# Small products of a linear-attention layer: full-width per tile, or in 32-column tiles once a sequence

## The chip, the cores and the metric

The kernel runs on one core of one Trainium2 chip. The metric is device time in microseconds; the profile is of one execution on that core. The engines are TensorE (PE in the rows; PEld is its weight load), VectorE (DVE), ScalarE (ACT), GpSimd (POOL) and SyncE (SP).

## What is computed

16 sequences of 512 tokens, width 256, float32, go through one layer: attention with 16 heads of width 16 and no softmax over positions, a residual and a layer norm, then a gated feed-forward network of width 704 with block-quantized weights and activations, again with residual and norm. The attention, cut to what matters:

```python
q = favor(x @ Wq + bq)          # per head: exp(x - max) / (sum + EPS)
k = favor(x @ Wk + bk)
v = x @ Wv + bv
numerator = einsum('bhld,bhmd->bhlm', q, k)
attention_probs = numerator / (sum(q) + EPS)
context = einsum('bhlm,bhmd->bhld', attention_probs, v)
return context @ Wo + bo
```

Since nothing nonlinear stands between the two einsums, a head's context is q times a 16x16 matrix, the sum over the sequence's tokens of k features by values. That matrix is what the change is about.

## The kernel before

Tokens are cut into 64 tiles of 128, four (T) to a sequence. Every engine runs one hand-written program: a loop over steps m, in each of which it does its share of several tiles, each of them at another stage; the order within a step is written out in code, and engines meet at semaphores only (`need(engine, semaphore, count)`). Attention runs in steps up to about 70, one tile a step; the preparation of the feed-forward weights runs beside it in 18 pieces; then the feed-forward loop (`ffn`) follows, starting while the last tiles of attention end.

A tile n in attention goes as follows. TensorE projects it to query and key (`query_key`, step n, 6 products of 512 columns in L820) and to values (6 of 256 columns). VectorE takes the head maxima (L682) and subtracts them (L720), ScalarE takes the exponential (L513) and re-seeds the PSUM bank with the bias (L449), VectorE sums and inverts (L692, L707), GpSimd multiplies into query and key features (L376). ScalarE copies the values out of PSUM (L540). In step n + 3 TensorE waits for features and values, transposes the 256 query features (L851, two transposes of 128 columns), and multiplies values by key features (L853): for each of two chunks of 128 features a product of 128 x 128 over the tile's 128 tokens, accumulated in the bank `pkv` over the four tiles. Only the blocks of 16 x 16 on the diagonal are of use. Once a sequence VectorE multiplies `pkv` by a mask that keeps them (L711, result `kv_m`), and TensorE multiplies that by Wo (L882), which ScalarE and VectorE split into two parts (L521, L696). In step n + 7 TensorE multiplies the transposed query features by the result (L820, 6 products into `wide`), and VectorE adds the residual (L667).

In VectorE's program L711 stands in step 4q + 5 for sequence q, ahead of the subtraction (L720) of that step's tile; in TensorE's, the last L853 of sequence q is in step 4q + 6, at its start, followed by a weight piece's transposes (L865) if there are any, the output projection of an earlier tile, `query_key`, L882 and the value projection.

Features (`feat`, query and key beside each other) and values (`v_sb`) have two buffers each. GpSimd (L375) and ScalarE (L539) wait with tile n until TensorE has ended the products of tile n - 2.

Of the kernel before, what the change touches and what calls it, by code (L numbers as in the profile page):

```python
# [32 lines left out]
P = 128  # L33
# [3 lines left out]
FEPS = 1e-6  # L37
LN_EPS = 1e-5
TINY = 1e-12
SHY = 1.0 + 2.0 ** -22  # L40
NEWTON = 3
BOWL = (4.0 / 3.0) ** 0.5
# [17 lines left out]
def layer_kernel(nc, x_tok, x_feat, Wq, bq, Wk, bk, Wv, bv, Wo, bo, w_ffn, I, out):  # L60
# [16 lines left out]
    with ExitStack() as ctx:  # L77
# [28 lines left out]
        wf_hi = sb("wf_hi", [P, KC, NW * P], F32R)  # L106
        wf_lo = sb("wf_lo", [P, KC, NW * P], F32R)

        SCRATCH = 15616
        scratch = sb("scratch", [P, SCRATCH])  # L110
        taken = [0]

# [16 lines left out]
        def cube(a, b):  # L129
            return part(a * b).rearrange("p (a b) -> p a b", a=a)  # L130


        w_qkv = part(KC * 3 * D).rearrange("p (c n) -> p c n", c=KC)
        xt_raw = [cube(KC, P) for _ in range(T)]
        feat = [part(2 * D) for _ in range(2)]
        prob = [part(2 * NH * (HD + 1)).rearrange("p (h e) -> p h e", e=HD + 1) for _ in range(2)]
        v_sb = [part(D) for _ in range(2)]
        hmax, hsum, hrec = ([part(2 * NH) for _ in range(2)] for _ in range(3))
        kv_m = cube(KC, P)
        until_post = taken[0]  # L140
# [64 lines left out]
        ld_xt = [sem(f"ld_xt{k}") for k in range(T)]  # L205
        ld_x = [sem(f"ld_x{k}") for k in range(T)]
        consts = sem("consts")
        wq_hi_s, wq_lo_s, opened = sem("wq_hi_s"), sem("wq_lo_s"), sem("opened")
        w_max, w_s2s, w_invs, w_xns, w_ys, w_mgs, w_cs, w_gs, w_qs, w_t, w_his, w_los = (
            sem(f"w_{k}") for k in "max s2 inv xn y mg c g q t hi lo".split())  # L210
        a_xhi, a_xlo, a_xbo, a_seed, a_vseed, a_qk, a_qkv, a_max, a_sub, a_exp, a_v, a_sum, a_rec, a_feat = (
            sem(f"a_{k}") for k in "xhi xlo xbo seed vseed qk qkv max sub exp v sum rec feat".split())
        a_post, a_qhi, a_qlo, a_kvm, a_c, a_chi, a_clo, a_out, a_res, a_sq, a_ln, a_x1 = (
            sem(f"a_{k}") for k in "post qhi qlo kvm c chi clo out res sq ln x1".split())
        e_max, e_s2s, e_invs, e_xns, e_ys, e_mgs, e_cs, e_gs, x_q = (
            sem(f"e_{k}") for k in "max s2 inv xn y mg c g q".split())
        x_t, x_hi, x_lo = sem("x_t"), sem("x_hi"), sem("x_lo")
# [46 lines left out]
        def run(eng, attention, ffn):  # L264

            for m in range(T * A_FROM, JOIN + T * B_TO):
                if m < T * A_TO:
                    attention(m)
                if m - JOIN >= T * B_FROM:
                    ffn(m - JOIN)  # L270

        def rows(m):
            return bass.ds(m * D, D)
# [62 lines left out]
        def _(pool):  # L336
# [20 lines left out]
            def attention(m):  # L357
                for n in tile(m - 5):
                    if n == 0:
                        pool.wait_ge(ld_wo, 32)  # L360
                    pool.wait_ge(ld_x[n % T], 16 * (n // T) + 16)
                    need(pool, a_res, n - T + 1)
                    pool.tensor_tensor(x_bo[n % T], x_in[n % T], bo_b[:, :], ALU.add).then_inc(a_xbo, 1)
                for j in pieces(m - 2):
                    need(pool, w_mgs, j + 1)
                    need(pool, w_gs, j)
                    pool.tensor_tensor(w_c, w_xn, w_mg[j % 2], ALU.add).then_inc(w_cs, 1)
                for j in pieces(m):
                    need(pool, w_invs, j + 1)
                    need(pool, w_cs, j)  # L370
                    need(pool, w_ys, j)
                    pool.tensor_tensor(blocks(w_xn), blocks(w_raw), over(w_inv, XB), ALU.mult).then_inc(w_xns, 1)
                for n in tile(m - 1):
                    need(pool, a_rec, n + 1)
                    need(pool, a_post, n - 1)  # L375
                    pool.tensor_tensor(heads(feat[n % 2]), prob[n % 2][:, :, 0:HD], over(hrec[n % 2], 2 * NH, HD),  # L376
                                       ALU.mult).then_inc(a_feat, 1)
                for j in pieces(m - PIECE_G):
                    need(pool, w_t, j)
                    need(pool, w_gs, j + 1)  # L380
# [55 lines left out]
        def _(act):  # L436
# [52 lines left out]
            def attention(m):  # L489
                if m % T == 0:  # L490
                    for n in tile(m - 4):
                        q_hi(n)
                for j in pieces(m - PIECE_T):
                    need(act, w_t, j + 1)
                    act.activation(wf_hi[:, :, bass.ds(j * P, P)], pc[:, 0:D].rearrange("p (c n) -> p c n", c=KC),
                                   ACT.Copy).then_inc(w_his, 1)
                for j in pieces(m - 1):
                    if j + 1 < NW:
                        need(act, w_max, j + 1)
                        need(act, w_xns, j + 1)  # L500
                        if j + 1 < NW - KC:
                            act.dma_start(w_raw, w_ffn[j + 1, :, :]).then_inc(ld_w, 16)
                        else:
                            act.dma_start(w_raw[:, 0:D - TAIL], w_ffn[j + 1, :, 0:D - TAIL]).then_inc(ld_w, 16)
                            act.dma_start(w_raw[:, D - TAIL:D], w_ffn[j + 1, :, D - P:D - TAIL]).then_inc(ld_w, 16)
                if m % T != T - 1:
                    for n in tile(m - 3):
                        q_hi(n)
                for g, n in ready(m, LN_A):
                    normalise(n, res[:, rows(n)], a_ln, LN_OPS * (g + 1), a_x1)  # L510
                for n in tile(m - 1):
                    need(act, a_sub, n + 1)
                    act.activation(prob[n % 2][:, :, 0:HD], prob[n % 2][:, :, 0:HD], ACT.Exp).then_inc(a_exp, 1)  # L513
                if m >= 1:
                    for n in tile(m + 1):
                        need(act, a_sub, n - 1)
                        seed(n)
                for q in seqs(m - 6):
                    need(act, a_c, q + 1)
                    need(act, a_out, T * q)  # L520
                    act.activation(c_hi[:, :, :], pc.rearrange("p (c n) -> p c n", c=KC), ACT.Copy).then_inc(a_chi, 1)  # L521
                for j in pieces(m - 2):
                    need(act, w_cs, j - 1)
                    need(act, w_gs, j - 1)
                    need(act, w_ys, j + 1)
                    act.activation(w_mg[j % 2], w_y, ACT.Copy, bias=FLOOR, scale=STEP).then_inc(w_mgs, 1)
                if m >= 0:
                    for n in tile(m + 2):
                        x_hi_step(n)
                for n, at in enumerate(SQUARE_AT):  # L530
                    if at == m:
                        squares(n, 0, a_res, a_sq)
                for j in pieces(m - 1):
                    need(act, w_mgs, j)
                    need(act, w_xns, j + 1)
                    act.activation(w_y, w_xn, ACT.Square, scale=BOWL).then_inc(w_ys, 1)
                for n in tile(m):
                    need(act, a_qkv, n + 1)
                    need(act, a_post, n - 1)  # L539
                    act.activation(v_sb[n % 2], pv[:, 0:D], ACT.Copy).then_inc(a_v, 1)  # L540
                for n in tile(m + 1):
                    if n > 0:
                        v_seed(n)
# [60 lines left out]

        @block.vector
        def _(dve):
            for k in range(3):
                cols = slice(k * D, (k + 1) * D)
                dve.wait_ge(wq_hi_s, k + 1)
# [36 lines left out]
            def attention(m):  # L646
# [59 lines left out]
                    need(dve, a_feat, n - 1)  # L706
                    dve.reciprocal(hrec[n % 2], hsum[n % 2]).then_inc(a_rec, 1)  # L707
                for q in seqs(m - 5):
                    need(dve, a_post, T * (q + 1))
                    need(dve, a_c, q)  # L710
                    dve.tensor_tensor(kv_m, pkv[:, 0:KC * P].rearrange("p (c n) -> p c n", c=KC),  # L711
                                      mask[:, :, :], ALU.mult).then_inc(a_kvm, 1)
# [101 lines left out]
        def _(pe):  # L814
# [27 lines left out]
            def attention(m):  # L842
                for n in tile(m - 3):
                    b = n % 2
                    need(pe, a_feat, n + 1)
                    need(pe, a_v, n + 1)
                    need(pe, a_qlo, n - 1)
                    if n % T == 0:
                        need(pe, a_kvm, n // T)
                    for c in range(KC):  # L850
                        pe.transpose(pqt[b][:, c * P:(c + 1) * P], feat[b][:, c * P:(c + 1) * P], ident[:, :])  # L851
                    for c in range(KC):
                        last = pe.matmul(pkv[:, c * P:(c + 1) * P], v_sb[b][:, c * P:(c + 1) * P],  # L853
                                         feat[b][:, D + c * P:D + (c + 1) * P],
                                         start=n % T == 0 and c == 0, stop=n % T == T - 1, skip_group_check=True)
                    last.then_inc(a_post, 1)
                if m % T == T - 1:
                    for n in tile(m):
                        query_key(n)
# [122 lines left out]
```

## Time and profile before

| | |
|---|---|
| median of 3 runs | 708.69 us (706.77 to 709.64) |
| the profiled execution | 707.44 us |
| its span, first to last instruction | 705.7 us |
| TensorE busy | 681.2 us, 97% of the span |
| VectorE, ScalarE, GpSimd busy | 627.4, 577.1, 562.0 us |
| mean granted TensorE clock | 0.995 |

Times in the rows are from the start of the span. A busy share is a mean over two stages; the attention stage lasts until about 255 us, the feed-forward stage from there to the end. Matmuls are pipelined and their ends are modelled: a row's duration is longer than the time until the next product may start.

### The profile page before, as it was taken

The numbers are of one execution on the slowest core, as the hardware profiler recorded it, in microseconds if no ns is written. First come the engines' busy times: TensorE is split into PE (matmuls) and PEld (weight loads), VectorE is DVE, ScalarE is ACT, GpSimd is POOL, SyncE is SP. The second block draws the span as 40 slices with busy tenths as digits, with TensorE's granted clock in tenths as the row PEclk, the third lists the DMA queues.
The fourth block names the chain that finished last, engine by engine and source line by source line (L and its number), as shares of the span: only waits on it lengthen the run. The fifth ranks groups of instructions, "written<-read, shape, count | busy, mean of one in ns | idle before, by whom it ended". The sixth has DMA issues, their size and how long they took to land.

```text
span 705.7 us, 16440 instructions
## 1 busy us (share of the span) xinstructions
PE 681.2 (97%) x4782; PEld 656.9 (93%) x4782; DVE 627.4 (89%) x1498; ACT 577.1 (82%) x1355; POOL 562.0 (80%) x581
## 2 busy tenths in 40 slices
PE   6999999999999979999999999999999999999993
PEld 5999999999998869999999999999999999999983
DVE  3999988999998989999999989989899998999874
ACT  5888888887778978898877777778777898888887
POOL 3778778788877878888888898888888888888760
PEclk9999999999999999999999999999999999999999
DMA  5323322223222100000000000000000011011114
GB/s 164 94 73 86 87 76 78 83 68 91 83 79 80 39 16 1 1 2 1 1 1 2 1 2 1 2 1 1 1 1 2 25 37 47 31 46 46 51 62 142
DMA packets 40473, 30.16 MB, mean 43 GB/s; under 512 B 3776, under 2 KB 40384, under 8 KB 40384
## 3 DMA queue, kind: packets, MB, share of 16 engines
q1 hardware_dynamic: 37648, 26.88, 12.7%
q10 hardware_dynamic: 2736, 2.23, 1.1%
q8 instruction: 39, 0.64, 0.4%
q14 instruction: 50, 0.41, 0.2%
HBM read 20.71 MB, written 8.39 MB: 41 GB/s over the span
## 4 chain that ended last, share of the span: by engine, by line
PE 88%; ACT 4%; DVE 3%; issue 3%; DMA 1%; POOL 1%; ACTq 0%; SPq 0%; DVEq 0%; POOLq 0%
PE bank L820 66%; PE wide L938 6%; PE wide L820 5%; PE bank L853 4%; PE bank L931 2%; PE bank L851 2%; PE wide L882 2%; PE bank L921 1%; PE bank L919 1%; DMA bias_b<-L_attn_bk 1%; ACT scratch L480 1%; PE wide L865 0%; ACT dump L475 0%; ACT res L480 0%; ACT bank L449 0%
## 5 line engine op out<-in xcount | busy, mean ns | idle before, releaser
L820 PE MATMUL bank<-wf_hi,rounded 128*128 128x352 f32 (+1 forms) x1664 | 387.0, 310 | 4.0 <-DVE res L768 1.7
L820 PEld LDWEIGHTS bank<-wf_hi,rounded 128*128 128x128 f32 x1664 | 283.9, 189 | 5.2 <-issue 3.9
L820 PE MATMUL bank<-wf_lo,rounded 128*128 128x352 f32 (+1 forms) x832 | 255.2, 307 | 0.0
L820 PEld LDWEIGHTS bank<-wf_lo,rounded 128*128 128x128 f32 x832 | 157.6, 189 | 0.0
L820 PE MATMUL bank<-qkv_hi,rounded 128*128 128x512 f32 (+1 forms) x512 | 146.4, 349 | 3.1 <-ACT bank L449 3.1
L416 POOL TENSOR_TENSOR scratch<-scratch 128x704 f32<-128x704 bf16 x64 | 94.9, 1482 | 38.9 <-DVE scratch L794 38.9
L820 PEld LDWEIGHTS bank<-qkv_hi,rounded 128*128 128x128 f32 x512 | 93.0, 191 | 14.2 <-issue 3.6
L405 POOL TENSOR_TENSOR scratch<-scratch 128x704 bf16<-128x704 f32 x64 | 98.3, 1536 | 1.9 <-ACT scratch L596 1.9
L376 POOL TENSOR_TENSOR scratch<-scratch 128x512 f32<-128x512 f32 x64 | 68.0, 1063 | 39.0 <-DVE scratch L707 38.8
L411 POOL TENSOR_TENSOR scratch<-scratch 128x704 f32<-128x704 f32 x64 | 89.3, 1395 | 3.7 <-DVE scratch L765 3.7
L820 PE MATMUL bank<-qkv_lo,rounded 128*128 128x512 f32 (+1 forms) x256 | 87.1, 340 | 0.0
L562 ACT ACTIVATE scratch<-bank 128x352 f32<-128x352 f32 x64 | 29.5, 462 | 52.1 <-PE bank L820 52.0
L475 ACT ACTIVATE dump<-res,row_sum 128x256 f32<-128x256 f32 x128 | 64.5, 504 | 0.9 <-DVE res L768 0.6
L802 DVE TENSOR_TENSOR rounded<-wide,rounded 128x768 fp32r<-128x768 f32 x64 | 60.6, 946 | 1.6 <-ACT rounded L575 1.6
L794 DVE TENSOR_TENSOR scratch<-scratch 128x704 bf16<-128x704 bf16 x64 | 58.4, 913 | 2.6 <-POOL scratch L405 2.6
L820 PE MATMUL wide<-rounded 128*128 128x256 f32 x384 | 59.9, 292 | 0.1
L587 ACT ACTIVATE scratch<-scratch 128x704 uint8<-128x704 f32 x64 | 50.3, 787 | 7.8 <-POOL scratch L411 7.0
L399 POOL TENSOR_TENSOR scratch<-scratch 128x256 f32<-128x256 bf16 x64 | 39.8, 622 | 20.2 <-DVE scratch L746 17.9
L575 ACT ACTIVATE rounded<-wide 128x768 fp32r<-128x768 f32 x64 | 52.0, 812 | 4.1 <-PE wide L938 0.2
L938 PE MATMUL wide<-ident,scratch 128*128 128x128 f32 x384 | 52.4, 273 | 2.0 <-POOL scratch L416 2.0
L820 PEld LDWEIGHTS bank<-qkv_lo,rounded 128*128 128x128 f32 x256 | 48.9, 191 | 4.6
L385 POOL TENSOR_TENSOR rounded<-scratch,rounded 128x256 fp32r<-128x256 f32 x64 | 47.2, 737 | 7.2 <-ACT rounded L446 7.2
(98 smaller groups left out, 1563.7 us busy)
## 6 DMA issues: line engine op xcount, KB each, us to landing
scratch<-x_feat SPq DMA_DIRECT2D x64, 128.0 KB, 2.2
scratch<-x_tok SPq DMA_DIRECT2D x64, 128.0 KB, 2.4
out<-scratch SPq DMA_DIRECT2D x64, 128.0 KB, 1.7
scratch<-w_ffn ACTq DMA_DIRECT2D x15, 128.0 KB, 2.3
scratch<-L_attn_Wq SPq DMA_DIRECT2D x1, 256.0 KB, 3.2
scratch<-L_attn_Wk SPq DMA_DIRECT2D x1, 256.0 KB, 3.4
scratch<-L_attn_Wv SPq DMA_DIRECT2D x1, 256.0 KB, 6.0
wo<-L_attn_Wo SPq DMA_DIRECT2D x1, 256.0 KB, 4.5
```

The source lines that it names most:

```text
L376: pool.tensor_tensor(heads(feat[n % 2]), prob[n % 2][:, :, 0:HD], over(hrec[n % 2], 2 * NH, HD), ALU.mult).then_inc(a_feat, 1)
L385: pool.tensor_tensor(xt_lo[n % T], xt_raw[n % T], xt_hi[n % T].bitcast(F32), ALU.subtract).then_inc(a_xlo, 1)
L405: pool.tensor_tensor(hc[n % 2], hxn[n % 2], hmg[n % 2], ALU.add).then_inc(h_c, 1)
L411: pool.tensor_tensor(blocks(hxn[n % 2]), blocks(hid[n % 2]), over(binv[n % 2], NB), ALU.mult).then_inc(h_xn, 1)
L416: pool.tensor_tensor(hq[n % 2][:, 0:I].rearrange("p (a c e) -> p a c e", a=11, e=BLK), hg[n % 2].rearrange("p (a c e) -> p a c e", a=11, e ...
L475: act.activation(dump[norm][:, :], res[:, rows(n)], ACT.Square, bias=row_sum[:, at], scale=-1.0 * D, accum_out=row_sq[:, at]).then_inc(sq, 1)
L575: act.activation(hqt_hi[n % 2][:, :, :], wide[:, 0:IP].rearrange("p (c n) -> p c n", c=IC), ACT.Copy).then_inc(h_hi, 1)
L587: act.activation(hy[n % 2], hxn[n % 2], ACT.Square, scale=BOWL).then_inc(h_y, 1)
L794: dve.tensor_tensor(hg[n % 2], hc[n % 2], hmg[n % 2], ALU.subtract).then_inc(h_g, 1)
L802: dve.tensor_tensor(hqt_lo[n % 2][:, :, :], wide[:, 0:IP].rearrange("p (c n) -> p c n", c=IC), hqt_hi[n % 2][:, :, :].bitcast(F32), ALU.su ...
L820: op = pe.matmul(dst, x(c), w(c), start=first and n == 0, stop=last and n == len(terms) - 1, skip_group_check=not first)
L938: last = pe.transpose(wide[:, c * P:(c + 1) * P], hq[n % 2][:, c * P:(c + 1) * P], ident[:, :])
```

## The change

The transposes of the query features stay where they are, in step n + 3. The products of values by key features leave that place. Once a sequence, in step 4q + 6 right behind the transposes of its last tile, TensorE now does them for all four tiles. A product of 128 x 128 is replaced by four of 32 x 32 on the diagonal (two heads each), which address the array as tiles of 128 rows by 32 columns at the positions 0, 32, 64 and 96; all contract over the 128 tokens as before. The bank `pkv` is cleared once by VectorE, as what lies off the diagonal is no longer written. Key features and values get six buffers (DEEP), query features keep two; GpSimd and ScalarE wait on the new semaphore `a_kv` in place of (ScalarE) or beside (GpSimd) `a_post`. Query and key features are no longer neighbours, so GpSimd writes them through a pattern with one more dimension; they lie over the raw weights, so the first of them waits until these are split (`wq_lo_s`).

```diff
-        feat = [part(2 * D) for _ in range(2)]
+        q_feat = [part(D) for _ in range(2)]
+        k_feat = [part(D) for _ in range(DEEP)]
...
-        v_sb = [part(D) for _ in range(2)]
+        v_sb = [part(D) for _ in range(DEEP)]
...
+                    if n == 0:
+                        pool.wait_ge(wq_lo_s, 3)
                     need(pool, a_rec, n + 1)
                     need(pool, a_post, n - 1)
-                    pool.tensor_tensor(heads(feat[n % 2]), prob[n % 2][:, :, 0:HD], over(hrec[n % 2], 2 * NH, HD),
+                    need(pool, a_kv, (n - DEEP) // T + 1)
+                    pool.tensor_tensor(features(n),
+                                       prob[n % 2][:, :, 0:HD].rearrange("p (s h) d -> p s h d", s=2),
+                                       over(hrec[n % 2], 2 * NH, HD).rearrange("p (s h) d -> p s h d", s=2),
                                        ALU.mult).then_inc(a_feat, 1)
...
-                    need(act, a_post, n - 1)
-                    act.activation(v_sb[n % 2], pv[:, 0:D], ACT.Copy).then_inc(a_v, 1)
+                    need(act, a_kv, (n - DEEP) // T + 1)
+                    act.activation(v_sb[n % DEEP], pv[:, 0:D], ACT.Copy).then_inc(a_v, 1)
...
+            dve.memset(pkv[:, 0:KC * P], 0.0).then_inc(zeroed, 1)
...
                 for q in seqs(m - 5):
-                    need(dve, a_post, T * (q + 1))
+                    need(dve, a_kv, q + 1)
...
-                        pe.transpose(pqt[b][:, c * P:(c + 1) * P], feat[b][:, c * P:(c + 1) * P], ident[:, :])
-                    for c in range(KC):
-                        last = pe.matmul(pkv[:, c * P:(c + 1) * P], v_sb[b][:, c * P:(c + 1) * P],
-                                         feat[b][:, D + c * P:D + (c + 1) * P],
-                                         start=n % T == 0 and c == 0, stop=n % T == T - 1, skip_group_check=True)
+                        last = pe.transpose(pqt[b][:, c * P:(c + 1) * P], q_feat[b][:, c * P:(c + 1) * P], ident[:, :])
                     last.then_inc(a_post, 1)
+                for q in seqs(m - 6):
+                    if q == 0:
+                        pe.wait_ge(zeroed, 1)
+                    need(pe, a_feat, T * (q + 1))
+                    need(pe, a_v, T * (q + 1))
+                    need(pe, a_kvm, q)
+                    for n in range(T * q, T * (q + 1)):
+                        for c in range(KC):
+                            for k in range(0, P, KVW):
+                                at = slice(c * P + k, c * P + k + KVW)
+                                last = pe.matmul(pkv[k:k + KVW, at], v_sb[n % DEEP][:, at], k_feat[n % DEEP][:, at],
+                                                 start=n % T == 0 and c == 0, stop=n % T == T - 1,
+                                                 skip_group_check=True, tile_position=(0, k))
+                    last.then_inc(a_kv, 1)
```

## Rows read from the trace of the kernel before

**Rows 1.** The page, parts 1, 2 and 5: engines, clock, GpSimd's feature product.

```profile
PE 681.2 (97%) x4782; PEld 656.9 (93%) x4782; DVE 627.4 (89%) x1498; ACT 577.1 (82%) x1355; POOL 562.0 (80%) x581
...
PEclk9999999999999999999999999999999999999999
...
L376 POOL TENSOR_TENSOR scratch<-scratch 128x512 f32<-128x512 f32 x64 | 68.0, 1063 | 39.0 <-DVE scratch L707 38.8
```

**Rows 2.** Windows: busy us and instructions of each engine, by stretch of attention.

```profile
core 0: us, PE busy (x) PEld busy (x) DVE busy (x) ACT busy (x) POOL busy (x), PEclk, DMA share, GB/s
0.00:40.00 40.00, 34.24 (x192) 30.00 (x193) 27.46 (x63) 28.18 (x66) 24.62 (x44) 0.96 0.42 120
60.00:75.00 15.00, 15.00 (x105) 13.87 (x104) 13.33 (x36) 12.99 (x37) 11.62 (x15) 1.00 0.27 80
...
210.00:225.00 15.00, 14.53 (x100) 13.08 (x99) 14.24 (x41) 12.64 (x34) 12.21 (x17) 1.00 0.29 80
```

**Rows 3.** Chain that ended last, one sequence: start us, us, what.

```profile
60.47 0.45 PE bank L853 x4
...
68.82 2.10 PE bank L820 x12
70.93 0.22 PE bank L851 x2
...
71.59 0.71 PE wide L820 x6
72.30 1.38 PE bank L820 x6
73.68 0.86 PE wide L882 x4
...
75.47 0.45 PE bank L853 x4
```

**Rows 4.** Groups by line and form: busy us, mean ns; idle before.

```profile
L853 PE MATMUL bank<-scratch 128*128 128x128 f32 x256 | 39.0, 275 | 0.0
```

**Rows 5.** Timeline, TensorE after it stood: start us, us, engine, line.

```profile
247.77 0.14 PEld L851 LDWEIGHTS bank<-ident,scratch 128*128 128x128 f32 x1 [1.59 <-POOL scratch L376]
...
247.83 0.14 PEld L851 LDWEIGHTS bank<-ident,scratch 128*128 128x128 f32 x1
...
254.72 0.14 PEld L931 LDWEIGHTS bank<-ident,scratch 128*128 128x128 f32 x1 [1.38 <-DVE rounded L643]
...
254.75 0.30 PE L931 MATMUL bank<-ident,scratch 128*128 128x128 f32 x1 [1.00 <-POOL scratch L399]
```

**Rows 6.** Timeline around the last products of a sequence, same columns.

```profile
69.16 1.06 POOL L376 TENSOR_TENSOR scratch<-scratch 128x512 f32<-128x512 f32 x1
...
70.98 0.61 PE L853 MATMUL bank<-scratch 128*128 128x128 f32 x4
...
72.09 0.36 DVE L711 TENSOR_TENSOR scratch<-bank,mask 128x256 f32<-128x256 f32 x1
...
72.37 0.68 DVE L720 TENSOR_TENSOR scratch<-bank,scratch 128x512 f32<-128x512 f32 x1
...
73.14 0.62 ACT L513 ACTIVATE scratch<-scratch 128x512 f32<-128x512 f32 x1
...
73.66 0.59 ACT L449 ACTIVATE bank<-bias_b 128x512 f32<-128x512 f32 x1
```

**Rows 7.** Timeline of the start, same columns as the timelines above.

```profile
5.18 1.41 DVE L610 TENSOR_TENSOR qkv_lo<-scratch,qkv_hi 128x512 fp32r<-128x512 f32 x2 [5.18 <-ACT qkv_hi L440]
...
9.40 0.77 PE L820 MATMUL bank<-qkv_hi,rounded 128*128 128x512 f32 x1 [2.73 <-ACT bank L449]
...
10.01 0.69 DVE L610 TENSOR_TENSOR qkv_lo<-scratch,qkv_hi 128x512 fp32r<-128x512 f32 x1 [3.42 <-ACT qkv_hi L440]
...
16.45 1.06 POOL L376 TENSOR_TENSOR scratch<-scratch 128x512 f32<-128x512 f32 x1 [1.86 <-DVE scratch L707]
```

**Rows 8.** Timeline of the last tile's transposes, same columns.

```profile
250.96 0.44 PE L851 MATMUL bank<-ident,scratch 128*128 128x128 f32 x2 [1.45 <-POOL scratch L376]
```

More of the change, by code:

```diff
@@ L39 @@
 TINY = 1e-12
+KVW = 32
+DEEP = 6
 SHY = 1.0 + 2.0 ** -22
@@ L107, in layer_kernel @@
         wf_lo = sb("wf_lo", [P, KC, NW * P], F32R)
-        SCRATCH = 15616
+        SCRATCH = 16128
         scratch = sb("scratch", [P, SCRATCH])
@@ L133, in layer_kernel @@
         w_qkv = part(KC * 3 * D).rearrange("p (c n) -> p c n", c=KC)
+        taken[0] = 0
+        q_feat = [part(D) for _ in range(2)]
+        k_feat = [part(D) for _ in range(DEEP)]
+        assert taken[0] >= KC * 3 * D
         xt_raw = [cube(KC, P) for _ in range(T)]
-        feat = [part(2 * D) for _ in range(2)]
         prob = [part(2 * NH * (HD + 1)).rearrange("p (h e) -> p h e", e=HD + 1) for _ in range(2)]
-        v_sb = [part(D) for _ in range(2)]
+        v_sb = [part(D) for _ in range(DEEP)]
         hmax, hsum, hrec = ([part(2 * NH) for _ in range(2)] for _ in range(3))
@@ L207, in layer_kernel @@
         consts = sem("consts")
+        zeroed = sem("zeroed")
         wq_hi_s, wq_lo_s, opened = sem("wq_hi_s"), sem("wq_lo_s"), sem("opened")
@@ L212, in layer_kernel @@
             sem(f"a_{k}") for k in "xhi xlo xbo seed vseed qk qkv max sub exp v sum rec feat".split())
-        a_post, a_qhi, a_qlo, a_kvm, a_c, a_chi, a_clo, a_out, a_res, a_sq, a_ln, a_x1 = (
-            sem(f"a_{k}") for k in "post qhi qlo kvm c chi clo out res sq ln x1".split())
+        a_post, a_kv, a_qhi, a_qlo, a_kvm, a_c, a_chi, a_clo, a_out, a_res, a_sq, a_ln, a_x1 = (
+            sem(f"a_{k}") for k in "post kv qhi qlo kvm c chi clo out res sq ln x1".split())
         e_max, e_s2s, e_invs, e_xns, e_ys, e_mgs, e_cs, e_gs, x_q = (
@@ L270, in run, with features @@
                     ffn(m - JOIN)
+        def features(n):
+            q_at, k_at = n % 2 * D, (2 + n % DEEP) * D
+            both = scratch[:, q_at:q_at + 2 * (k_at - q_at)].rearrange("p (s x) -> p s x", s=2)[:, :, 0:D]
+            return both.rearrange("p s (h d) -> p s h d", d=HD)
         def rows(m):
@@ L845, in attention @@
                     need(pe, a_feat, n + 1)
-                    need(pe, a_v, n + 1)
                     need(pe, a_qlo, n - 1)
-                    if n % T == 0:
-                        need(pe, a_kvm, n // T)
                     for c in range(KC):
-                        pe.transpose(pqt[b][:, c * P:(c + 1) * P], feat[b][:, c * P:(c + 1) * P], ident[:, :])
-                    for c in range(KC):
-                        last = pe.matmul(pkv[:, c * P:(c + 1) * P], v_sb[b][:, c * P:(c + 1) * P],
-                                         feat[b][:, D + c * P:D + (c + 1) * P],
-                                         start=n % T == 0 and c == 0, stop=n % T == T - 1, skip_group_check=True)
-                    last.then_inc(a_post, 1)
+                        last = pe.transpose(pqt[b][:, c * P:(c + 1) * P], q_feat[b][:, c * P:(c + 1) * P], ident[:, :])
+                    last.then_inc(a_post, 1)
+                for q in seqs(m - 6):
[12 more added lines that the diff above has]
+                    last.then_inc(a_kv, 1)
                 if m % T == T - 1:
```

## The prediction

> **What bounds the kernel now.** I read the page first. TensorE holds the largest share of the span, VectorE comes second, and TensorE's clock is granted in full nearly throughout [rows 1]. An average can mislead over two stages, so I went on to the windows by stretch. While attention runs alone, TensorE is busy all of the 15.00 us of nearly every stretch (14.53 in one), with VectorE at 13.3 to 14.2 us beside it; larger gaps come on TensorE only in the last tiles, as the 1.45 us at 250.96 [rows 2, 8]. A busy matmul row can hide waiting, since the ends are modelled, so the third view is the chain that ended last, cut to one sequence [rows 3]. It never leaves TensorE. Each piece starts where the last ended, and the same four-tile pattern returns after 15.00 us (75.47 less 60.47). The pieces are full work: 0.22 us of transposes and 0.45 us of values by key features for each tile, 0.71 of output projection and 2.10 of query, key and value projections (1.38 for query and key, so 0.72 for the values), and once a sequence 0.86 us at L882; a weight piece, one every four tiles, has two transposes as L851 has, 0.22 us. Four times (0.22 + 0.45 + 0.71 + 2.10) is 13.92, plus 0.86 and 0.22 is 15.00, so nothing is left over for waiting. Every us put on or taken off TensorE in this stage is therefore a us of the kernel, sixteen times, until another engine takes over; VectorE would, once 0.8 to 1.7 us are gained a sequence [rows 2]. The later, feed-forward stage is not touched.
>
> **What the change removes.** The four products of a tile (two calls, recorded as two products each: 256 for 128 calls [rows 4]) take 0.45 us, 0.112 us each; four tiles give 16 products and 1.80 us a sequence [rows 3]. All of it is on the path.
>
> **What it adds.** A tile now has eight calls, each of 32 weight columns and 32 streamed columns. If a call is still recorded as two products, that is 16 a tile and 64 a sequence, each with a weight load of its own, in one burst at one place. What a pair (load and product) of that size costs no row shows; the bounds come from larger ones. A product of 128 streamed columns follows the last after 0.112 us, the one at L882 with 256 after 0.86 / 4 = 0.215 [rows 3]: the cost goes with the columns, so 32 would stream in 0.028 us, a quarter of 0.112. I take its load to shrink with the columns too. That is one end for tiles that go one after the other: 64 x 0.028 = 1.8 us, exactly what was removed. If four tiles in different columns really run at once, the array needs a quarter of this, 0.45 us. The other end is a pair as long as now, 0.112 us: 64 x 0.112 = 7.2 us. Between them stands the one view in which TensorE had been idle, so that nothing was queued in the array [rows 5]: a load begins at 247.77 and the next at 247.83, with a product between them, and at 254.72 and 254.75 a load and its product start 0.03 us apart. So a pair is handed over in 0.06 us, and no two pairs in the trace are closer. The loads there are of 128 columns, and part of the 0.06 may be their own work; but 0.03 from a load to its product, after a wait, looks like the rate at which instructions arrive. At that rate the array, however it is divided, starves: 64 x 0.06 = 3.84 us, of which 0.2 may be handed over while the transposes ahead run (0.22 us [rows 3]), so 3.64 us. I take this value, because it is from the rows nearest to a stream with little work in each instruction.
>
> Then the array changes from one tile to four column tiles and back. The trace has no such change. Lower bound nothing; upper bound one emptying each way, what a product lasts beyond its share of the stream, 0.275 - 0.112 = 0.16 us [rows 4], so 0.33 us. I take one, 0.17 us.
>
> The Trainium skill, TensorE: Matmul & The Clock Gate, section on packing small matmuls, says that tiles at different positions start about 4 ns apart and run together. No row here shows it; by that alone, with the array as the limit, the burst would be short and the change a gain (the second rival below). The same page, section on the back-to-back issue gap, speaks against the change: starts never come closer than about 25 ns however few the columns, and without hardware decode about 62 ns a matmul. By 62 ns the burst would be 64 x 0.062 = 4.0 us, by 25 ns for load and product each 3.2 us; my 3.64 lies between. TensorEngine Tiling, section on key properties, says that a change of tiling mode drains the engine, and no row here shows it.
>
> **The sum.** A sequence: -1.80 + 3.64 + 0.17 = +2.01 us. Fifteen sequences lie in the stretch where TensorE hardly waits: 15 x 2.01 = +30.2. The last is different: TensorE has idled before it [rows 8], so the products taken from its last tiles save nothing but the final 0.45, and the burst stands between the last features and the start of the feed-forward on VectorE: 3.64 + 0.17 - 0.45 = +3.4. Together +33.6 us. The profiled execution took 707.44 us (span 705.7): 741.0 us. The median of the runs is 708.69, 0.2% above it, so my figure is 741 us with that much play.
>
> **What else moves.** (1) VectorE's masking (L711) now waits for the burst, and in VectorE's queue the next tile's subtraction (L720) is behind it, for which ScalarE's exponential (L513) and seed (L449) wait. Today L711 starts 0.50 us after the last product ends (70.98 + 0.61 to 72.09) [rows 6], so it will start some 3.3 us later than now. After the burst TensorE has 0.71 + 1.38 + 0.86 + 0.72 + 0.22 = 3.9 us of other work [rows 3] before it needs the seed; L711, L720, L513 and L449 take 0.36 + 0.68 + 0.62 + 0.59 = 2.3 us [rows 6]. Covered, 1.6 us to spare. (2) But VectorE can't work in the stall. A sequence would be 13.2 us of other TensorE work and 3.8 of burst; VectorE has 13.3 to 14.2 us to do, nearly all in the 13.2. In the dense sequences I allow up to 0.4 us each, 6 us in all, in the range and not in the sum. (3) The product at L882 needs the masked result 0.71 + 1.38 = 2.1 us after the burst, as it does now [rows 3]; L711 takes 0.36. (4) ScalarE's value copy (L540) no longer waits for the tile before last; but nobody waits for that copy while TensorE never idles: nothing; in the last tiles, where TensorE waits for GpSimd [rows 8], nothing either. (5) The feature product on GpSimd (L376) writes through a pattern with one dimension more. It takes 1063 ns and GpSimd stands 38.8 us in all before its 64 instances, 0.6 us each [rows 1]. Up to that much more is hidden where TensorE sets the pace, and I expect no more than the 1.06 us, since the elements are as many: nothing. (6) Its first one waits for the last weight split, which ends at 10.70, and started at 16.45 anyway [rows 7]; the clearing of the PSUM bank goes into 5.18 us in which VectorE idled [rows 7]. Without that cover the clearing would cost about what L711 takes for as many columns, 0.36 us, once. No DMA is added or moved.
>
> **Rivals.** *No pair cost but streaming* (the small products keep the array's rate, one after the other): 64 x 0.028 + 0.17 - 1.80 = +0.2 us a sequence, +3 in all, 710 us. For it: TensorE runs full before the burst and might have instructions queued. Against: the last features come late (GpSimd's L376 runs from 69.16 to 70.22, the transposes that wait for them start at 70.93 [rows 3, 6]), so there is only 0.7 us in which to queue. *Faster: the four column tiles run at once.* Then the burst is 0.45 to 0.9 us, and TensorE gains 0.7 to 1.2 us a sequence after 0.17 us for the change of mode; VectorE's 13.3 to 14.2 us end it at about 0.8 in the fuller sequences. 15 x 0.8 = -12: 695 us. It decides as soon as a pair costs under 0.025 us, (1.80 - 0.17) / 64. Against it speaks that no two instructions of TensorE stand that close after a wait [rows 5]. *Load and product do not overlap* inside a small tile, so that each pair costs what the large ones cost, 0.112 us: 7.2 + 0.17 - 1.8 = +5.6 us a sequence, +91 in all, 798 us. Against: the loads are shorter by columns. *The clock falls* after a burst of nearly empty work. The granted clock was 0.96 over the first 40 us, in which TensorE stood 2.73 us before its first product of 512 columns, and full through the gaps near 250 us [rows 1, 2, 7, 8]. A mean of 0.96 is 0.08 of 40 us, 3.2 us, at 1.2 in place of 2.4 GHz. If each burst brought such a stretch it would cost 1.6 us: 741 + 15 x 1.6 = 765 us. TensorE isn't idle in the burst, so I give it little.
>
> **How the numbers follow.** The forecast, pairs of 0.045 to 0.075 us: 0.52. Streaming rate alone: 0.12. Tiles at once: 0.16. No overlap, 0.075 us and up: 0.14. Clock: 0.06. The forecast's own range is 16 sequences of pairs from 0.045 (2.9 us, +1.3 a sequence, 728) to 0.075 with VectorE's 6 us (about 766). For 8 in 10 I go down to the gain, 695, and up to 778, and leave out the upper part of the no-overlap case (0.10) and a little on the other side. A measurement of this kernel tells about 0.5%, 3.5 us, from no change. Faster by more: 0.16; within: 0.11; slower by more: 0.73.
>
> **What would show it.** Products at the new line: 1024 of them, with 1024 loads, in 16 bursts; a burst of 3.6 us confirms the pair cost, 1.8 or less refutes it. Between bursts the chain should still be all TensorE, with 13.2 us of other work and a period near 17.0. VectorE should idle some 3 us before L711 each time. If the bursts are short and the period is still near 15, VectorE is the bound. The prediction is wrong if a call isn't recorded as two products, since the count then halves.

## The result

The changed kernel took 703.50 us (median of 8 runs, 702.73 to 704.18) against 706.99 us of the kernel before (8 runs, 705.73 to 709.64): a ratio of 0.9949, 95% interval 0.9936 to 0.9961. It is faster by 0.5%, while I had forecast 741 us, and the forecast was wrong. The profiled execution took 704.18 us.

The page of the changed kernel, parts 1 and 2, and from its groups by line and form the new products; they answer to [rows 1, 4]:

```profile
PE 675.6 (96%) x5550; PEld 641.4 (91%) x5550; DVE 627.4 (89%) x1499; ACT 574.5 (82%) x1355; POOL 561.2 (80%) x581
...
PEclk9999999999999979999999999999999999999998
...
L878 PE MATMUL bank<-scratch 128*32 128x32 f32 x1024 | 12.5, 202 | 0.0
```

There are 1024 small products, two to a call as foreseen, and 768 more instructions than before; yet TensorE is busy 5.6 us less. The granted clock is new in two places: a 7 at about a third of the span, and an 8 in the last slice, where TensorE's work has ended.

The timeline of one sequence's burst (start us, us, engine line, what, count, idle before):

```profile
68.53 0.38 PE L866 MATMUL bank<-ident,scratch 128*128 128x128 f32 x2
68.84 0.65 PEld L878 LDWEIGHTS bank<-scratch 128*32 128x32 f32 x64 [0.17 <-issue]
68.84 0.76 PE L878 MATMUL bank<-scratch 128*32 128x32 f32 x64
```

64 products span 0.76 us, and the last of them lasts 0.20. So 63 steps take 0.56 us: 0.009 us for a load and a product, where I had 0.06. (A call is still recorded as two products.) The load side stands 0.17 us before the burst, on nothing that the profile shows.

The product with Wo (L882 before, L907 now) comes once a sequence and serves as the clock for the period. In the kernel before, then in the changed one, two of them six sequences apart and the last but one of the stage (timeline, same columns):

```profile
58.52 1.02 PE L882 MATMUL wide<-wo,scratch 128*128 128x256 f32 x4
...
148.54 1.02 PE L882 MATMUL wide<-wo,scratch 128*128 128x256 f32 x4
...
239.50 1.02 PE L882 MATMUL wide<-wo,scratch 128*128 128x256 f32 x4
```

```profile
71.74 1.02 PE L907 MATMUL wide<-wo,scratch 128*128 128x256 f32 x4
...
159.38 1.02 PE L907 MATMUL wide<-wo,scratch 128*128 128x256 f32 x4
...
232.83 1.02 PE L907 MATMUL wide<-wo,scratch 128*128 128x256 f32 x4
```

The period was (148.54 - 58.52) / 6 = 15.00 us and is (159.38 - 71.74) / 6 = 14.61 us. TensorE was relieved of 1.80 us a sequence and given 0.56 us of products; 0.39 us came out of it. The last period of the stage went the other way: from the last but one of these products to the last are 13.22 us before (239.50 to 252.72) and 14.58 now (232.83 to 247.41). The part on the end of the stage comes back to it. The question for the experiments is where the rest is. The windows of the changed kernel show that TensorE now has gaps and that VectorE isn't full either, and below them the clock (compare [rows 2]):

```profile
core 0: us, PE busy (x) PEld busy (x) DVE busy (x) ACT busy (x) POOL busy (x), PEclk, DMA share, GB/s
60.00:75.00 15.00, 14.86 (x153) 13.06 (x153) 13.65 (x36) 13.21 (x38) 11.98 (x16) 1.00 0.29 81
...
240.00:255.00 15.00, 9.76 (x102) 7.94 (x103) 11.47 (x31) 10.40 (x30) 11.46 (x15) 0.73 0.07 19
```

The chain of the changed kernel over one period (start us, us, what). Before, it never left TensorE [rows 3]; now it leaves it once a sequence, between 61.2 and 65.4 us:

```profile
60.46 0.73 PE wide L838 x6
...
61.28 0.09 DVE res L685
...
62.56 0.71 DVE scratch L710
...
63.35 0.32 DVE scratch L725
...
63.74 0.12 POOL scratch L391
...
64.76 0.62 POOL scratch L398
...
65.43 0.44 PE wide L890 x2
65.87 0.72 PE wide L838 x6
66.59 2.10 PE bank L838 x12
68.69 0.22 PE bank L866 x2
68.91 0.69 PE bank L878 x50
```

This is a loop through three engines. The output projection in TensorE's step 4q + 3 (60.46) releases VectorE's residual (L685), on which VectorE stands 0.97 us; in VectorE's queue follow the two reductions (L700, L710) and the reciprocal (L725) of that step; GpSimd then makes the features (L391) and, behind them, the scaled weight piece (L398), and TensorE waits for these in step 4q + 5, at the piece's transposes (L890). From the end of the projection's stream (60.30 + 6 x 0.117 = 61.01 in the timeline) to L890 at 65.43 are 4.42 us. TensorE's own work in this stretch is 0.71 + 0.22 + 0.71 + 2.10 + 0.22 = 3.96 us; the 0.46 us between them is waiting. In the kernel before it held 2 x 0.45 more, 4.86 us. If the loop took its 4.42 us there too, which that kernel's chain can't show since TensorE covers it, it was covered by 0.44 us, and taking the products out uncovered it.

### The profile page after: what moved, and what is told of

The parts are those of the page before. It is cut to its first block, busy times and chain, and to the rows that moved or that the text cites. A ratio compares the mean times of both kernels' runs of the same rounds, so it can differ in the third digit from the quotient of the medians.

```text
span 702.5 us, 17973 instructions
## 1 busy us (share of the span) xinstructions
PE 675.6 (96%) x5550; PEld 641.4 (91%) x5550; DVE 627.4 (89%) x1499; ACT 574.5 (82%) x1355; POOL 561.2 (80%) x581
## 4 chain that ended last, share of the span: by engine, by line
PE 77%; issue 7%; DVE 6%; ACT 3%; POOL 3%; SPq 1%; DMA 1%; ACTq 0%; POOLq 0%; DVEq 0%
PE bank L838 59%; PE wide L963 6%; PE wide L838 4%; PE wide L907 2%; PE bank L956 2%; DVE scratch L710 2%; PE bank L878 2%; POOL scratch L398 1%; PE bank L946 1%; PE bank L944 1%; PE bank L866 1%; PE wide L890 1%; DVE scratch L725 1%; POOL scratch L391 1%; DVE res L685 1%
## 5 line engine op out<-in xcount | busy, mean ns | idle before, releaser
L391 POOL TENSOR_TENSOR scratch<-scratch 128x512 f32<-128x512 f32 x64 | 68.0, 1063 | 33.1 <-DVE scratch L725 32.8
L838 PEld LDWEIGHTS wide<-rounded 128*128 128x128 f32 x384 | 51.5, 192 | 2.4 <-issue 0.6
L530 ACT ACTIVATE scratch<-scratch 128x512 f32<-128x512 f32 x64 | 40.2, 628 | 15.5 <-DVE scratch L738 14.7
```

What stands on the lines that cost most here:

```text
L391: pool.tensor_tensor(features(n), prob[n % 2][:, :, 0:HD].rearrange("p (s h) d -> p s h d", s=2), over(hrec[n % 2], 2 * NH, HD).rearrange( ...
L838: op = pe.matmul(dst, x(c), w(c), start=first and n == 0, stop=last and n == len(terms) - 1, skip_group_check=not first)
```

## The experiments

**What a small product costs, and why.** Four runs change only the burst.

e1_w128 and e3_w64 change the tile width, e2_serial the order:

```diff
-KVW = 32
+KVW = 128      # e3_w64: 64
```

```diff
-                    for n in range(T * q, T * (q + 1)):
-                        for c in range(KC):
-                            for k in range(0, P, KVW):
+                    for k in range(0, P, KVW):
+                        for n in range(T * q, T * (q + 1)):
+                            for c in range(KC):
```

> The changed kernel with the products of values by key features as full 128 x 128 ones again, but still in one burst a sequence and with the six buffers (16 products in place of 64). If the small tiles are what shortens TensorE's work: a burst of 16 x 0.112 = 1.8 us, a period of 15.0 us a sequence and about 707 us, as before the change. If batching and buffers are what helps: about 703 us.

> The changed kernel with the same 64 small products in another order: all 16 of column tile 0, then the 16 of the next, and so on, so that neighbours never lie in different column tiles. If four tiles running at once is the cause of 0.009 us a pair: the burst grows to 64 x 0.028 = 1.8 us or more, the period by about 1.1 us, the time to some 718 us. If a small product is simply cheap, wherever it lies: burst 0.76 us as now, 703 us.

> The changed kernel with tiles of 64 columns, two at once, 32 products a sequence. If pairs run at once and cost what their columns cost: each group of two takes 0.056 us, the burst 16 x 0.056 = 0.9 us plus the fixed part, about 1.1 us. If the hand-over of instructions limits (0.009 us an item as now): 0.3 us plus the fixed part, shorter than now.

e5_nokv leaves one call of the 32 in each burst:

```diff
-                    for n in range(T * q, T * (q + 1)):
...
+                    pe.matmul(pkv[0:KVW, 0:KVW], v_sb[(T * q) % DEEP][:, 0:KVW], k_feat[(T * q) % DEEP][:, 0:KVW],
+                              start=True, stop=True, skip_group_check=True, tile_position=(0, 0)).then_inc(a_kv, 1)
```

> The changed kernel with 63 of the 64 small products of each burst left out (one call is left, so that the array still changes its tiling; the attention result is not the reference's). The three bursts measured so far give a period of 14.03 us plus the length of the burst with small tiles, 13.71 us plus the burst with full ones. If that is the law, and the burst counts in full: 14.05 us. If other engines set the period of the changed kernel: it stays at 14.6 us.

One burst from the timeline of each, e1_w128, e2_serial, e3_w64 in this order (a fence each, same columns):

```profile
72.73 1.95 PE L878 MATMUL bank<-scratch 128*128 128x128 f32 x16
```

```profile
72.15 1.91 PE L878 MATMUL bank<-scratch 128*32 128x32 f32 x64
```

```profile
69.52 1.15 PE L878 MATMUL bank<-scratch 128*64 128x64 f32 x32
```

| | products | us a product | burst | period | period less burst | time |
|---|---|---|---|---|---|---|
| changed kernel | 64 of 32 columns, 4 tiles in turn | 0.009 | 0.58 | 14.61 | 14.03 | 703.50 |
| e2_serial | 64 of 32 columns, one tile after the other | 0.027 | 1.74 | 15.76 | 14.02 | 719.14 |
| e3_w64 | 32 of 64 columns, 2 tiles in turn | 0.030 | 0.95 | 15.00 | 14.05 | 707.66 |
| e1_w128 | 16 of 128 columns, whole array | 0.112 | 1.79 | 15.51 | 13.72 | 716.97 |
| e5_nokv | 2 of 32 columns | | 0.06 | 14.09 | 14.03 | 698.59 |

Beside these runs the kernel before took 707.1 to 707.9 us (medians). A product's cost is the span less the last product's own time (0.20 to 0.28 us) over the steps between, the period is from the same product with Wo six sequences apart. Three things follow. First, a small product of one column tile streams at 0.027 us, a quarter of 0.112, as bounded; in turn over four column tiles it costs 0.009, a third of that, with the same 64 instructions. So the tiles do run at once, and it is the order of the calls that lets them: e2_serial, in the wrong order, is slower than the kernel before. Of the two expectations for e3_w64 the one by columns came nearer: 0.95 us, against 1.1 us by columns and 0.5 us by the number of instructions. Second, period less burst is the same 14.03 us for every burst of small tiles, from 0.06 to 1.74 us long: the burst is paid in full, and VectorE sets no bound above 14.1. Third, with full tiles it is 13.72. The difference, 0.31 us, is there in each of the four runs in which the array changes its tiling, and I take it as the price of the change, there and back.

I had expected about 707 us for e1_w128 if tiling was all; it took 716.97 (ratio 1.012, interval 1.009 to 1.015). The same products as before at the same 0.112 us, but in one place, cost 0.5 us more a sequence than spread over the tiles. That fits the loop's wait: in the weight loads' view TensorE waits for GpSimd at L890 3.4 us in ten sequences in this run, as in the changed kernel.

**Where the freed time is lost.** Two runs add the same piece of work, 0.43 us of TensorE's time, in two places.

```diff
+                if 7 <= m < NT and m % T == 0:                      # e13_free: behind the transposes
+                    pe.matmul(pkv[:, D:2 * D], ident[:, :], mask[:, :, :], start=True, stop=True, skip_group_check=True)
...
                     last.then_inc(a_c, 1)
+                    if m < NT:                                      # e14_paid: step 4q + 6, behind L907
+                        pe.matmul(pkv[:, D:2 * D], ident[:, :], mask[:, :, :], start=True, stop=True, skip_group_check=True)
```

> The changed kernel with one added plain product of 256 columns (0.43 us of TensorE's time, into the unused half of the products' PSUM bank) in every step 4q+4, that is between the output projection of step 4q+3 and the waits of step 4q+5. Loop theory: TensorE waits 0.5 us there anyway, so the added work is nearly free: period 14.61 to 14.7 us, 704 us. If TensorE's sum of work counts everywhere: 15.04 us, 710 us.

> The same added product, 0.43 us, in step 4q+6 behind the product at L907, outside that stretch. Both theories: paid in full, period 15.04 us, 710 us. It is there for the comparison with the run before it: the difference of place is the loop's.

Product with Wo in e13_free, then in e14_paid (timeline, same columns):

```profile
73.68 1.02 PE L909 MATMUL wide<-wo,scratch 128*128 128x256 f32 x4
...
161.28 1.02 PE L909 MATMUL wide<-wo,scratch 128*128 128x256 f32 x4
```

```profile
72.78 1.02 PE L907 MATMUL wide<-wo,scratch 128*128 128x256 f32 x4
...
162.99 1.02 PE L907 MATMUL wide<-wo,scratch 128*128 128x256 f32 x4
```

Periods of 14.60 and 15.03 us; 704.33 and 708.14 us, one execution each. In the changed kernel work in step 4q + 4 costs nothing, the same work in step 4q + 6 its full 0.43 us. The periods carry this and not the times: from the first product with Wo to the last are 219.4 and 225.8 us, but that first product comes at 29.86 and at 27.66 us, which hides 2.2 of the 6.4 us. TensorE's waits in the weight loads' view between 60 and 210 us (ten sequences; who waited for whom, us in total, times, longest), of the changed kernel and of e13_free, agree:

```profile
PEld wide L890 <- POOL scratch L398: 3.4, 9, 0.4
PEld bank L878 <- issue: 1.7, 10, 0.2
PEld bank L866 <- POOL scratch L391: 0.4, 1, 0.4
```

```profile
PEld bank L878 <- issue: 1.7, 10, 0.2
```

In e13_free the filler has taken the place of the waits for GpSimd; what stays is the change of tiling. In e14_paid they are there as in the changed kernel.

If so, part of the products belongs into that stretch. e4_pertile puts them behind each tile's transposes, e8_half behind every second tile's:

```diff
-                    for n in range(T * q, T * (q + 1)):
+                for n in tile(m - 3):                # e4_pertile: this tile's 8 calls, four times a sequence
...
+                    if n % 2 == 0:                   # e8_half: 16 calls of tiles n - 1 and n, twice a sequence
+                        continue
```

> The changed kernel with the small products right behind the transposes of each tile again, 16 a step in place of 64 once a sequence. Theory of the loop (TensorE's step 4q+3, VectorE, GpSimd, TensorE's step 4q+5 sets the period, so work in these two steps is free up to about 0.45 us and work outside counts in full): half of the products move into the free place, the other half cost 2 x (0.14 + change of mode), so the period is 14.61 - 0.78 + 2 x 0.3 = 14.4 us, the time about 700 us. If TensorE's sum of work sets the period: two more to four more changes of mode at 0.17 us each, 15.1 us, 711 us.

> The changed kernel with two bursts of 32 small products a sequence, behind the transposes of the second and the fourth tile. Theory of the loop: the first burst lies in the stretch where TensorE waits 0.5 us now, so of its 0.28 + 0.33 us only 0.1 is paid; the second costs 0.61 in place of 0.90: period 14.61 - 0.29 + 0.1 = 14.42 us, 700.6 us. Rival, TensorE's sum of work with an unavoidable 0.5 us wait: one more change of tiling, 14.61 + 0.33 = 14.94 us, 708 us.

e4_pertile: period 14.98 us, 709.19 us (ratio 1.0014, 0.9997 to 1.0031), near the figure of the sum of work. Four changes of tiling at 0.31 us and four times 16 x 0.009 are 1.8 us, and 13.20 + 1.8 = 15.0: they fill the free stretch and more. I had priced a change, there and back, at 0.16 to 0.2 us when I wrote 14.4. e8_half: period 14.36 us as foreseen (14.42), and 702.25 us (ratio 0.9921, 0.9895 to 0.9946), 1.6 more than foreseen. Most of that is noise: the kernel before took 707.65 us beside this run and 706.99 beside the changed kernel, and the two ratios differ by 0.0028, 2.0 us, where 2.9 were foreseen.

e6_piece6 tries to take the wait away at its other end, by moving what waits: the transposes of the first twelve weight pieces and their copies one step later.

```diff
-                for j in pieces(m - PIECE_T):
+                for j in turned(m):      # at + PIECE_T + (at < 47) == m, on TensorE, ScalarE and VectorE
```

> The changed kernel with the transposes of the first twelve weight pieces, and their copies on ScalarE and VectorE, one step later. Theory of the loop: TensorE waits 0.33 us a sequence at these transposes for GpSimd's product, in the step before the burst's; with them a step later that wait is gone while the 0.12 us before the feature transposes stays: period 14.28 us, 12 x 0.33 = 4 us less, 699.5 us. Rival, VectorE as the bound (it is busy 13.3 to 14.8 of 15 us): the wait moves elsewhere, period 14.6, 703.5 us.

It took 708.03 us (ratio 0.9997, 0.9983 to 1.0012), period 14.93 us: worse, and neither theory had it. Its chain between two sequences never leaves TensorE, but pieces there are longer than their work:

```profile
66.64 0.36 PE bank L870 x2
67.01 0.87 PE wide L842 x6
67.88 2.32 PE bank L842 x12
70.20 0.40 PE bank L870 x2
...
71.29 0.37 PE wide L894 x2
...
73.76 1.06 PE wide L911 x4
```

The same pieces are 0.22, 0.71, 2.10, 0.22, 0.22 and 0.86 us elsewhere; small waits of 0.14 to 0.22 us, 1.05 in all, have replaced one of 0.33. The transposes now stand in the step of the product with Wo, which uses the same PSUM tile and waits for their copies (L680 on VectorE ends at 73.57, L911 starts at 73.72). In the weight loads' view between 60 and 210 us, the loads of L911 stand 2.7 us in seven sequences, and those of L842 1.6 us in nine for GpSimd's L406. Which of these waits causes the others I didn't settle.

**What is given back at the end of the attention stage.** From the last product with Wo to the transposes of the third feed-forward tile (L931, L956) nothing was changed, and from there to the end both kernels take 441.0 us. In the kernel before, then in the changed one (timeline, same columns):

```profile
252.72 1.03 PE L882 MATMUL wide<-wo,scratch 128*128 128x256 f32 x4
...
264.72 0.38 PE L931 MATMUL bank<-ident,scratch 128*128 128x128 f32 x2
```

```profile
241.13 0.44 PE L866 MATMUL bank<-ident,scratch 128*128 128x128 f32 x2 [1.71 <-POOL scratch L391]
...
244.32 0.69 PE L866 MATMUL bank<-ident,scratch 128*128 128x128 f32 x2 [1.45 <-POOL scratch L391]
...
247.41 1.91 PE L907 MATMUL wide<-wo,scratch 128*128 128x256 f32 x4
...
261.48 0.39 PE L956 MATMUL bank<-ident,scratch 128*128 128x128 f32 x2
```

From the last product with Wo to the third tile are 12.00 us against 14.07; L907 itself takes 1.91 us in place of 1.03. The windows of the changed kernel there:

```profile
core 0: us, PE busy (x) PEld busy (x) DVE busy (x) ACT busy (x) POOL busy (x), PEclk, DMA share, GB/s
239.00:242.00 3.00, 0.93 (x7) 0.52 (x5) 2.92 (x9) 3.00 (x9) 2.69 (x5) 1.00 0.17 46
242.00:244.00 2.00, 0.88 (x6) 0.67 (x6) 1.97 (x6) 2.00 (x7) 1.74 (x3) 0.86 0.28 66
244.00:246.00 2.00, 1.68 (x67) 1.28 (x67) 1.50 (x4) 1.29 (x5) 2.00 (x3) 0.50 0.00 0
...
254.00:256.00 2.00, 2.00 (x8) 2.00 (x8) 0.28 (x1) 0.00 (x0) 1.38 (x4) 0.50 0.03 8
```

The granted clock fell to 1.2 GHz at about 243.4 us. TensorE had stood 1.71 us before the transposes at 241.13 and was in the second wait, the 1.45 us before 244.32. The clock came back at 250.3 and was low once more from 253.7 to 257.1, some 10 us together, and that met the last burst, the product with Wo and the first feed-forward products. Over the 8 runs the mean granted clock was 0.988 to 0.993, and 0.989 to 0.998 over the executions of the kernel before that ran beside the experiments; the mean doesn't say where it fell. The kernel before has nearly the same gaps, 1.38 us before 247.77 and 1.45 before 250.96 [rows 8], and its clock stayed up there. Two things differ: it has 0.45 us of values by key features behind each of these transposes, and the changed kernel has a further wait of 0.36 us between the two.

The loss begins before this stretch, in the last period: 14.58 us in the changed kernel, and 13.40 in e7_fill, whose clock is full there, so some 1.2 us. And it isn't the same in each execution. In e14_paid, with waits of 1.72 and 1.45 us at the same places, the clock was low for 3.4 us only, and the stretch took 11.90 us; in e13_free it was low for 6.8 us and the stretch took 12.42. The 2.1 us are therefore what this one execution lost.

e7_fill puts products of no use, on constants and into a free bank, into these gaps:

```diff
             def attention(m):
+                if m in (NT + 1, NT + 2):
+                    need(pe, a_v, NT)
+                    for _ in range(3):
+                        pe.matmul(pv[:, 0:D], ident[:, :], mask[:, :, :], start=True, stop=True)
```

> The changed kernel with three filler products of 256 columns (1.3 us together) before each of the last two tiles' transposes, where TensorE stands 1.7 and 1.5 us; they write a PSUM bank that is free then. If the fall of the granted clock to 1.2 GHz at 243.4 us, for 10.2 us in all, costs what the next steps took longer (2.3 us between the last product at L907 and the second feed-forward tile): clock 0.996 or more and about 701.2 us. If the stretch waits for the other engines anyway: 703.5 us with the clock up.

It took 702.43 us (4 runs; ratio 0.9920, 0.9889 to 0.9952), an interval that overlaps the changed kernel's, so this run alone decides little. Its trace says more: the same stretch took 13.34 us, the first fall was gone, and one remained, of 3.4 us between 252 and 256. e12_half_fill has both, two bursts and the filler:

> Two bursts of 32 a sequence (period 14.37 us measured) together with the filler products before the last two tiles' transposes. If the two gains add, 15 x 0.24 = 3.6 us of period and about 1 us of clock: 699.5 us, against 703.5 of the changed kernel and 707.3 of the one before. If the start and the clock's phase take it back: 702 us, as with the two bursts alone.

Its windows of that time (same columns), and the two marks of the stretch:

```profile
244.00:248.00 4.00, 2.75 (x47) 2.03 (x37) 3.81 (x11) 2.91 (x9) 3.54 (x6) 1.00 0.00 0
248.00:252.00 4.00, 2.66 (x19) 2.48 (x18) 3.30 (x9) 2.54 (x8) 3.49 (x5) 1.00 0.01 4
```

```profile
245.22 1.03 PE L914 MATMUL wide<-wo,scratch 128*128 128x256 f32 x4
...
257.21 0.38 PE L963 MATMUL bank<-ident,scratch 128*128 128x128 f32 x2
```

The clock stays up, the stretch takes 11.99 us, as before the change, and the period is 14.36 us. It took 699.30 us (4 runs, 698.33 to 700.81), ratio 0.9884 (0.9865 to 0.9903): faster than both kernels, its interval clear of the changed kernel's 0.9936 to 0.9961. e8_half, which differs from it by the filler alone, had the clock low from 241.9 to 252.1 us, a stretch of 13.46 us and a last period of 14.35 against 13.47. So the filler gave back 1.5 and 0.9 us there. That is no reason for e8_half's 1.6 us over its expectation, which was reckoned from the changed kernel, and that has the fall too.

**The buffers alone.** e11_deep_only keeps six buffers, the split features and the earlier release of the value copy, and puts full 128 x 128 products back into each tile's step.

> The changed kernel with full 128 x 128 products in every tile's step as in the kernel before; what is left of the change is the six buffers, the split features and the earlier release of the value copy. If buffers do nothing while TensorE never waits: period 15.00 us and the time of the kernel before, 707.3 us. If the released copy on ScalarE helps: under 705 us.

707.72 us, ratio 0.9999 (0.9988 to 1.0010), period 15.00. They do nothing for the time; they are what makes the burst possible.

## Why the prediction was wrong

The 3.2 us between the two profiled spans (705.7 and 702.5) are: 0.6 us at the start (first product with Wo at 28.5 and 27.9 us); 15 periods, 224.2 against 219.5 us, 4.7 us; 2.1 us given back at 12.00 against 14.07; nothing after that. The 0.6 us can't be put down to the change: that first product lies anywhere from 27.7 to 30.1 us in the other runs' traces, and between 10 and 20 us the mean granted clock was 0.87 in the kernel before and full in the changed one. The 4.7 us are 6.04 gained in the first 14 periods, less the 1.36 by which the last one grew.

- *Every us put on or taken off TensorE in attention is one of the kernel, until VectorE takes over.* Right for most of the period: e14_paid shows that 0.43 us more cost 0.43. Wrong for what is taken off between the projection of step 4q + 3 and the piece's transposes of step 4q + 5: 0.90 us left that stretch and some 0.44 were gained, because the loop through VectorE and GpSimd then sets it (e13_free: 0.43 us put there cost nothing). The chain of the kernel before shows the path that was longest and not by how much.
- *A pair costs 0.06 us.* This step failed, and it alone turned the sign: with 0.58 us of burst in place of 3.64, the same sum is -1.05 us a sequence and about 692 us. I took two instructions 0.03 us apart, in an engine that had been idle, for the rate at which instructions arrive. They arrive at least as fast as 0.009 us a pair in the burst. I also misread the rows: the 0.03 us is from 254.72 alone, and at 247.77, in the same view, the product begins with its load, as the line below shows. What is left is the 0.06 us from one load of 128 columns to the next, and how much of that is the load's own work no run here separates. The rows had one other reading, that the burst is limited by the array, and I ranked it lower on a single pattern.

```profile
247.77 0.33 PE L851 MATMUL bank<-ident,scratch 128*128 128x128 f32 x1 [1.38 <-POOL scratch L376]
```

- *No pair in the trace is closer, so the array starves.* No instruction in the trace had so little work, so no row could have been closer. The lack of a case is not a limit.
- *The change of tiling, 0.17 us.* Mis-sized: 0.31 us a burst, near the upper bound of 0.33 that I gave.
- *VectorE stalls at the masking, up to 0.4 us a sequence.* It hung on the long burst and went with it.
- *The rival "tiles at once", 695 us, deciding under 0.025 us a pair.* The mechanism and the deciding point were right (0.009 decides for it, e2_serial's 0.027 against it). Its price was wrong: I let VectorE's busy time end the gain at 0.8 us a sequence. The gain was 0.39, ended by a loop of waits with no engine full: 1.80 - 0.58 - 0.31 - 0.52 = 0.39, where the 0.52 is 13.72 less the 13.20 us of TensorE's other work. Of it the loop's waits are 0.46; for the other 0.06 I have no row.
- *The clock.* I priced a fall after each burst; none came there. It came at the stage's end, in gaps that were nearly all there already, and took some 3 us of the profiled execution, 1.2 of the last period and 2.1 behind it.
- *Nothing from the value copy, the pattern, the clearing.* Right: e11_deep_only.

## What to carry to other kernels

Small products in different column tiles overlap only if consecutive calls go to different tiles; count their cost as an array shared, plus a fixed price each time the tiling changes, and batch them for that reason. When an engine that fills every us is relieved, look in its chain at which stretches the work is taken from: where a loop through the other engines takes nearly as long, only its slack is gained there, and work that must run somewhere belongs in that stretch. A gap of TensorE that was harmless can still cost the clock; check the granted clock behind each one after a change.

## What the runs showed of the hardware

- A float32 product of 32 x 32 over 128 rows, as recorded (two to a call) and with its load, takes 0.009 us in turn over four column tiles and 0.027 us in one tile (64 x 64 in turn over two: 0.030; 128 x 128: 0.112). The Trainium skill, TensorE: Matmul & The Clock Gate, has about 25 ns as the least distance in its section on the back-to-back issue gap; e2_serial agrees, and the burst over four tiles goes under it, as the Trainium skill's section on packing small matmuls says it can (it gives about 4 ns a tile). The 62 ns that the Trainium skill gives there for issue without hardware decode is not seen.
- Changing the array's tiling and back costs 0.31 us in a running stream (14.03 less 13.72 us); the load side stands 0.17 us before the burst. The Trainium skill, TensorEngine Tiling, key properties, says that the change drains the engine; the runs show a price that fits this, and not the emptying itself.
- The clock fell to 1.2 GHz within the second of two gaps of 1.7 and 1.5 us in the changed kernel, for 6.8 us, and once more for 3.4; at the same gaps it was low for 3.4 us in all in e14_paid, and it did not fall at gaps of 1.4 and 1.5 us in the kernel before. With 1.3 us of useless products in each gap it fell once, for 3.4 us, in one kernel (e7_fill) and not at all in another (e12_half_fill), so what such a gap costs can't be read from its length.
